# Q and K of the next batch inside the attention loop, scores in 64-row tiles with the mask as a matmul, and plain maxima

## What is computed

```python
xn = layernorm(x)
q, k, v = xn @ Wq + bq, xn @ Wk + bk, xn @ Wv + bv         # 16 heads of 16
scores = where(band & valid, q @ kc.T / 4, -1e9)            # 64 queries x 192 keys per block
a = softmax(scores) @ vc @ Wo + bo
h = layernorm(a + xn) * g1 + b1
t = layernorm(gelu(h @ W1 + c1) @ W2 + c2 + h) * g2 + b2
chosen = argmax(xn @ gate_w.T)
out = x + t + xn + xn @ expert_w[chosen].T
```

## Time and profile before

| | |
|---|---|
| three runs | 1550.31 us median, 1548.87 to 1557.77 |
| profiled execution, first to last instruction | 1553.1 us |
| TensorE busy | 1240.9 us, 80% |
| VectorE busy | 1071.5 us, 69% |
| ScalarE, GpSimd busy | 739.8 us, 739.9 us, 48% each |
| mean granted TensorE clock | 0.913 of full |
| DMA | 135 MB, mean 87 GB/s |

### The profile page before, as it was taken

The page is one execution under the profiler, slowest core; times in us unless marked ns, Lnnn a source line. Parts: engine busy times, 40 slices in busy tenths (PEclk is TensorE's granted clock), DMA queues, the critical chain, the costliest instruction groups (busy, mean ns, idle before and its releaser), DMA issues.

```text
span 1553.1 us, 34323 instructions
## 1 busy us (share of the span) xinstructions
PE 1240.9 (80%) x10696; PEld 714.8 (46%) x10696; DVE 1071.5 (69%) x3743; ACT 739.8 (48%) x1356; POOL 739.9 (48%) x749
## 2 busy tenths in 40 slices
PE   0648885999678985999859997689858898599967
PEld 0424452735346353654527454373535535265435
DVE  8656775777757775867757677576766676587565
ACT  1305744366543744447443565426544374445642
POOL 6443745156531766037550474406752177504661
PEclk9959997999989997989979899798988899799979
DMA  7463056220733119130462206422082212912010
GB/s 237 92 139 118 3 117 122 76 92 29 144 79 100 57 69 166 50 112 13 108 131 69 99 8 145 91 83 83 33 156 75 88 57 74 162 48 94 2 28 28
DMA packets 89647, 135.00 MB, mean 87 GB/s; under 512 B 10209, under 2 KB 62305, under 8 KB 87393
## 3 DMA queue, kind: packets, MB, share of 16 engines
q1 hardware_dynamic: 83328, 115.91, 30.0%
q0 software_dynamic: 6144, 16.79, 4.4%
HBM read 74.47 MB, written 59.90 MB: 87 GB/s over the span
## 4 chain that ended last, share of the span: by engine, by line
PE 49%; DMA 17%; issue 11%; POOL 8%; DVE 8%; SPq 3%; ACT 3%; DVEq 0%; POOLq 0%; ACTq 0%
DMA pair_dram<-pool 9%; PE bank L1132 8%; PE bank L1035 8%; PE bank L1154 8%; PE bank L1036 7%; PE bank L1038 7%; PE bank L1181 6%; DMA q_s<-q_s 5%; DVE xn L604 2%; SPq L284 2%; DMA ys_dram<-xn 2%; PE bank L1102 2%; POOL x_sb L453 2%; POOL x_sb L451 2%; POOL rs L386 2%
## 5 line engine op out<-in xcount | busy, mean ns | idle before, releaser
L713 DVE CUSTOM_DVE_ANT_0 bank<-bank,mask 128x192 f32<-128x192 f32 x1024 | 337.3, 388 | 199.1 <-PE bank L1132 195.1
L943 ACT ACTIVATE pool<-bank 128x512 f32<-128x512 f32 x512 | 293.0, 597 | 118.9 <-PE bank L1154 113.2
L1132 PE MATMUL bank<-k_s,q_s 128*64 128x192 f16 x2048 | 175.3, 269 | 144.1 <-DMA q_s<-q_s 141.2
L440 POOL TENSOR_SCALAR_AFFINE_SELECT pool<-pool 128x512 f32<-128x512 f32 x256 | 172.2, 675 | 194.1 <-ACT pool L943 193.4
L1154 PE MATMUL bank<-q_s,k_s 128*128 128x256 f16 x1024 | 199.3, 290 | 28.7 <-issue 21.3
L389 POOL TENSOR_TENSOR rs<-ve,neghalf 128x1 f32<-128x1 f32 x64 | 36.9, 577 | 384.8 <-DVE ve L776 384.8
L1132 PEld LDWEIGHTS bank<-k_s,q_s 128*64 128x64 f16 x2048 | 77.8, 113 | 250.1 <-issue 226.9
L1181 PE MATMUL bank<-pool,v_a 128*32 128x256 f32 (+2 forms) x2560 | 161.1, 345 | 19.9 <-DVE pool L727 8.6
L989 ACT ACTIVATE pool<-bank,c1c 128x512 f32<-128x512 f32 x128 | 87.8, 686 | 169.5 <-PE bank L1038 132.5
L790 DVE TENSOR_TENSOR pool<-pool 128x512 f16<-128x512 f32 x128 | 106.7, 839 | 63.3 <-ACT pool L955 62.2
L713 DVE DVE_READ_ACCUMULATOR2_ANT m_sb<- 128x1 f32 x1024 | 144.6, 141 | 0.3
(11 more groups left out here) (149 smaller groups left out, 2511.1 us busy)
## 6 DMA issues: line engine op xcount, KB each, us to landing
pair_dram<-pool SPq DMA_DIRECT2D x32, 512.0 KB, 7.6
xn<-xs_dram SPq DMA_DIRECT2D x40, 384.0 KB, 3.7
ys_dram<-xn SPq DMA_DIRECT2D x120, 128.0 KB, 1.7
q_s<-pair_dram SPq DMA_DIRECT2D x48, 256.0 KB
k_s<-pair_dram SPq DMA_DIRECT2D x48, 256.0 KB
x_sb<-in_L_attn_x SPq DMA_DIRECT2D x8, 1024.0 KB, 5.7
res_dram<-x_sb SPq DMA_DIRECT2D x8, 1024.0 KB, 4.8
res_r<-res_dram SPq DMA_DIRECT2D x8, 1024.0 KB, 7.4
```

The costliest lines, as they stand in the source:

```text
L440: nc.gpsimd.affine_select(out=p, in_=p, compare_op=ALU.is_ge, fill=0.0, base=0, pattern=[[0, 4], [1, 2 * W]], channel_multiplier=-1).then_ ...
L713: ins = nc.vector.tensor_tensor_reduce(out=SB[u % 2][:, i * WIN:i * WIN + WIN], in0=SB[u % 2][:, i * WIN:i * WIN + WIN], in1=mask[:, v, :] ...
L943: nc.scalar.activation(prob[:, (k + 2) % 3, 2 * pu:2 * pu + 2, :], TB[u % 2][:, :].rearrange("p (h q) -> p h q", h=2), ACT.Exp, scale=EXP_ ...
L1132: mm = nc.tensor.matmul(SB[u % 2][W * bl:W * bl + W, i * WIN:i * WIN + WIN], q_s[:, h, W + w0:2 * W + w0], k_s[:, h // 2, w0:w0 + WIN], st ...
```

## The change

- The x of the next batch is loaded in the previous turn (after the 11th sorted tile), its statistics stand in steps 0 to 4, the normalization in steps 8 to 11, its transposes in steps 11 to 14.
- Q and K of b + 1 are computed in steps 15 to 30: three of a unit's six matmuls in each step, between the two halves of the transposed scores; high part by ScalarE and low part by VectorE at every second step. They use two banks instead of four.
- The host permutes the columns of Wq, Wk and their biases; stores to pair_dram write every copy (12 of 256 KB instead of 4 of 512 KB), loads take 48 rows each (8 of 384 KB instead of 12 of 256 KB), in two halves by heads with a semaphore each. The copy of the row q_s<-q_s is gone.
- q_s holds two heads in 128 rows as k_s does. Scores and transposed scores contract over 48 or 64 rows; heads are grouped by row half (par) instead of by pair (pu). In a half step the transposed scores of one row half alternate with the scores of the other.
- The mask is added by two more matmuls for each half step (64 rows, 256 columns, from an identity), and the maximum is one plain reduction of 384 columns for two heads.
- The column transposes of the maxima use the banks of the scores, and wait for all maxima issued so far.

```diff
-    XN_AT = 23
+    XN_AT = 8
+    XT_AT = XN_AT + 3
+    QK_AT = XT_AT + 4
-    pair_dram = nc.dram_tensor("pair_dram", (2, 4, P, S), F16, kind="Internal").ap()
+    pair_dram = nc.dram_tensor("pair_dram", (2, 2, 4, 2, 3, HD, S), F16, kind="Internal").ap()
+    MAX_STEPS = [LEAD - T + 3] + [T * g + MAX_AT - 1 + LEAD for g in range(G - 2)]
-        q_s = sb("q_s", [P, H, S + 2 * W], F16)
+        q_s = sb("q_s", [P, H // 2, S + 2 * W], F16)
-        QB, VB = TB + MB, OB + TB
+        QB, VB = MB, OB + TB
...
+            def pair_stores(b, i):
+                c, qk = divmod(i, 2)
+                for src, done, slots in ((qk_h, qk_hi, (0, 2 if qk else 1)), (qk_l, qk_lo, (1 if qk else 2,))):
+                    sp.wait_ge(done.sem, done.at(b, 2 * i + 2))
+                    for slot in slots:
+                        sp.dma_start(pair_dram[c, qk, :, :, slot, :, :].rearrange("j a d s -> d (j a) s"),
+                                     src[:, 2 * qk + c, :]).then_inc(pair_st[i % 2].sem, 16)
+            def stack_loads(b, i, first=False):
+                c, qk = divmod(i, 2)
+                if not first and qk == 0:
+                    sp.wait_ge(ST_ps.sem, ST_ps.at(b - 1, 4 * T * (c + 1)))
+                    sp.sem_inc(passed, 1)
+                sp.wait_ge(pair_st[i % 2].sem, pair_st[i % 2].at(b, 48 * (i // 2 + 1)))
+                dst = k_s if qk else q_s
+                for a in range(2):
+                    sp.dma_start(dst[W * a:W * a + KW, 4 * c:4 * c + 4, W:W + S],
+                                 pair_dram[c, qk, :, a, :, :, :].rearrange("j o d s -> (o d) j s")).then_inc(stack[c].sem, 16)
...
+            def turn(b, last, x_next=True):
                 max_rows(b, 1)
+                load_res(b)
+                max_rows(b, 2)
                 if not last:
+                    pair_stores(b + 1, 0)
+                max_rows(b, 3)
                 if not last:
+                    pair_stores(b + 1, 1)
+                    for i in range(2):
+                        stack_loads(b + 1, i)
+                    for i in range(2, 4):
+                        pair_stores(b + 1, i)
+                    for i in range(2, 4):
+                        stack_loads(b + 1, i)
                     store_res(b + 1)
+                    sorted_tiles(b + 1, x_next)
                 store_out(b)
...
             def maxima(b, j):
+                for n, par in enumerate((1, 0)):
+                    dve.wait_ge(S_ps.sem, S_ps.at(b, 2 * j + n + 1))
+                    dve.sem_inc(passed, 1)
+                    nc.vector.tensor_reduce(m_sb[:, 4 * g + par:4 * g + 4:2, t],
+                                            SB[par][:, 0:2 * WIN].rearrange("p (h c) -> p h c", h=2), AX.X, ALU.max).then_inc(mx.sem, 1)
...
+            def score_mm(out, n, j, par, i):
+                g, t = divmod(j, T)
+                h, r = 2 * g + i, slice(W * par, W * par + KW)
+                q = W + (2 * t + n) * W
+                return nc.tensor.matmul(out[W * n:W * n + W, i * WIN:i * WIN + WIN], q_s[r, h, q:q + W], k_s[r, h, q - W:q + 2 * W],
+                                        start=i == 0, stop=False, skip_group_check=True)
...
+            def mask_mm(out, n, t, par):
+                r = slice(W * par, W * par + W)
+                band = mask[r, edge(2 * t + n), :, :].unsqueeze(1).broadcast_to([W, 2, 2, W])
+                dst = out[W * n:W * n + W, 0:2 * WIN].rearrange("p (h c k) -> p h c k", h=2, c=3)[:, :, 0::2, :]
+                return nc.tensor.matmul(dst, ident16[r, :], band, start=False, stop=True, skip_group_check=True)
...
+            def max_cols(b, g, issued):
+                pe.wait_ge(mx.sem, mx.at(b, 2 * issued))
+                nc.tensor.transpose(SB[g % 2][0:4 * T, 0:P], m_sb[:, 4 * g:4 * g + 4, :].rearrange("p h t -> p (h t)"),
...
+            def scores_t(b, k, par):
+                j = k - 1 + LEAD
+                both = 1 <= k and j < STEPS
...
+                if both:
+                    scores_wait(b, j, 1 - par)
                 for i in range(2):
+                    mt = score_t_mm(TB[par], k, par, i)
+                    if both:
+                        for n in range(2):
+                            score_mm(SB[1 - par], n, j, 1 - par, i)
+                mt.then_inc(ST_ps.sem, 1)
+                if both:
+                    for n in range(2):
+                        ms = mask_mm(SB[1 - par], n, j % T, 1 - par)
+                    ms.then_inc(S_ps.sem, 1)
...
             def turn(b, last):
                 for k in range(STEPS + LAG):
+                    for par in range(2):
                         if k < STEPS:
+                            scores_t(b, k, par)
+                        if par == 0 and XT_AT <= k < XT_AT + 4 and not last:
+                            xn_transposes(b + 1, k - XT_AT)
+                        if par == 0 and QK_AT <= k < QK_AT + 16 and not last:
+                            qk_half(b + 1, *divmod(k - QK_AT, 2))
                     if k >= LAG:
                         values(b, k - LAG)
```

More of the change, by code:

```diff
@@ L267, in load_x @@
                 sp.dma_start(x_sb[:, :, :], x_v[b]).then_inc(x_in.sem, 16)
-            def stacks(b):
[L271 to L288, removed]
@@ L499, in turn @@
                     band(b, k)
-                    if k == XN_AT - 1 and not last:
+                    if k == TH + 1 and not last:
                         rstd(b + 1, 0, ve0, rs0)
@@ L829, in turn @@
                         maxima(b, k - 1 + LEAD)
-                    if k == 2 * T + MAX_AT and not last:
+                    if k < TH and not last:
+                        for t in range(2):
+                            c1_tile(b + 1, 2 * k + t)
+                    if k == TH and not last:
                         c1_stage(b + 1)
@@ L848, in _ @@
             assert done == N_PREP_Z
+            for t in range(T):
+                c1_tile(0, t)
             c1_stage(0)
@@ L854, in _ @@
                 xn_low(0, u)
+            for u in range(8):
+                qk_low(0, u)
             dve.wait_ge(pprep.sem, N_PPREP_V)
@@ L1003, in _ @@
                 xn_high(0, u)
-            c2_stage(0)
+            for u in range(8):
+                qk_high(0, u)
             weights_b()
@@ L1048, in xn_transposes @@
                 pe.wait_ge(xn_rdy.sem, xn_rdy.at(b, TH * (u // DC) + TH))
-                if u == 0 and not first:
-                    pe.wait_ge(mT_ev.sem, mT_ev.at(b - 1, G))
                 if u >= 2:
@@ new lines, in scores @@
+            def scores(b, j, first=False):
+                for par in (1, 0):
+                    scores_wait(b, j, par, first)
+                t = j % T
+                for i in range(2):
+                    for n in range(2):
+                        for par in (1, 0):
+                            score_mm(SB[par], n, j, par, i)
+                for n in range(2):
+                    for par in (1, 0):
+                        mm = mask_mm(SB[par], n, t, par)
+                        if n == 1:
+                            mm.then_inc(S_ps.sem, 1)
@@ L1299, in _ @@
             pe.wait_ge(prep.sem, N_PREP_A)
+            for u in range(8):
+                for part in range(2):
+                    qk_half(0, u, part)
             c2_stage(0, True)
@@ L1350 @@
             a = a.transpose(0, 2, 1)
+        if name[8:] in ("Wq", "bq", "Wk", "bk"):
+            a = a.reshape(-1, P // HD, HD).swapaxes(1, 2).reshape(a.shape)
         if name[8:] in ("bq", "bk", "g1", "c1"):
```

227 lines of the change are left out of this document (114 added, 113 removed).

## The result

The changed kernel takes 1935.15 us (median of 4, 1910.83 to 1952.26), the kernel before 1552.62 us beside it (median of 4, 1548.87 to 1557.77). Two of the four runs (1947.54 and 1952.26 us) are slow ones and the ratio leaves them out: 1.2351, 95% interval 1.2289 to 1.2414. I had forecast 1484 us, range 1425 to 1600. The sign was wrong and the time lies far outside the range. The profiled execution (the run of 1922.77 us) has a span of 1921.0 us against 1553.1, and a mean granted clock of 0.752 against 0.913.

What follows compares the result with a forecast made beforehand. It took TensorE to bound the loop and the first scores' DMA wait to leave a hole behind it. Seven turns -56, last turn -6, prologue -4: -66 us from 1553.1, forecast 1484 us, range 1425 to 1600.

Steps and rivals of the forecast that it cites:

- The half step: In the attention loop: transposed scores (T) hide scores (S) on the opposite row half; 0.44 us against the present 0.61.
- my upper bound of 0.89: Half step in microseconds if every change of tile shape costs 0.10 us, including one from scores to masks.
- rival A: Loop: every tile-shape change is paid, also between row halves; half step 0.89 us, total 1609 us, slower; chance 0.27.
- B: Loop: shape changes half paid, 0.05 us each; half step 0.70, total about 1550 us, no change; chance 0.15.
- a fixed three steps: Loop steps 1 to 3 at the low clock: 0.74 us a half step against 1.00, 6 x -0.26 = -1.6 us.
- +13.9 us: Loop: normalization +4.1, transposes +1.5, Q and K +3.0 and +8.8, less 3.5 for work leaving the end.
- Steps 15 to 18: Loop: three Q and K products a step, 0.75 us with the change of shape; +3.0 us together.
- steps 8 to 14: Loop: next batch's normalization in steps 8 to 11, +4.1 us; transposes of x in steps 11 to 14, +1.5.
- the steps with Q and K alone: Loop steps 19 to 30: TensorE needs 1.97 us a step against 1.24 now, 12 x 0.73 = +8.8 us.
- Behind the loop: Loop end to W2: hole and QK products gone, GpSimd's adds hold VectorE; W2 starts 16 us earlier a turn.
- Rival C: Behind the loop: GpSimd's adds don't meet GELU's low parts; W2 9 us a turn earlier, total 1421 us; chance 0.12.
- -8 us a turn: Net of one turn: loop +8.7, behind the loop -16, W1 and W2 stages -0.5; seven turns -56 us.

Runs made afterwards that it cites:

- run 16: Changed kernel with transposed scores, scores and masks no longer interleaved; scores and masks over 128 rows, only transposed scores over 64: 1701.14 us.
- run 1: Changed kernel with each half step's two transposed scores issued first, then four scores, then two masks, still 64 and 48 rows: 1910.38 us, ratio 1.2264.
- run 2: Changed kernel with transposed scores, scores and masks not interleaved and all over 128 rows, zeros in the other head's rows: 1638.14 us, ratio 1.0517.
- run 13: Changed kernel without its new scores: Q and K in the loop, scores over 128 rows, masks on VectorE; 1571.29 us, ratio 1.0114.

## Why the prediction was wrong, point by point

**The half step, the step that failed.** "I take the lower: [...] those that share no part of the array start side by side", 0.44 us. It measured 1.46. Two errors lie in it. The first was the overlap: changes of shape are paid between row halves as well, four in a half step, and T hides nothing of S. A change costs nearly the same time at both levels, some 0.12 us: the kernel before has 0.61 and 1.00 us a half step, which is 0.37 and 0.75 for the columns and 0.24 and 0.25 for two changes, and run 16 shows the same. So at 2.4 GHz this half step would be 0.92 to 0.98 us, 0.48 of columns and 0.44 to 0.50 of changes; that is an estimate, as no run has this order at 2.4 GHz. It lies above my upper bound of 0.89 (whose terms add up to 0.91, with a change from S to M that doesn't exist): rival A came, not the forecast and not B, and by A's own sum this error alone makes the kernel slower. I had a row for column halves only the earlier trace rows and carried it over to rows. On this the Trainium skill's page "TensorEngine Tiling (Array Packing)" (Key Properties), with its drain at each change of mode, was the one that agrees with the trace, and I named it and took the other.
The second was not in the text at all: every term of the sum, both bounds and all the rivals held the loop's clock at 2.4 GHz from step 4 on. The low level of the first steps stood in the earlier trace rows and in the 0.89 of the earlier trace rows, and I priced it as a fixed three steps. In the changed kernel it lasts into steps 19 to 22 in five of the seven turns, into step 31 in the other two, and into step 23 in the last turn. Runs 1 and 2 price it: loops of 848.3 us with 64 and 48 rows, 563.8 with 128 rows and the same order, so 284 us. Why few rows keep the clock down no run shows. The interleaving costs another 62 us (910.2 to 848.3). The remaining 115 us of the +461 are those that run 2 has over the kernel before: the terms of Q and K, and the mask products.

**The rest of the loop.** Right in the main, once the half step is left out. I had put +13.9 us for normalization, transposes and Q and K less what leaves the end, and +1.5 for the maxima's transposes. In run 13, which has the half step of before, the loop takes 70.8 us against 57.8 in the fourth turn: +13. Steps 15 to 18 were put at +3.0 and cost 3.1; steps 8 to 14 at 5.6 together and cost 6.4 in four turns and 4.9 to 5.0 in three; the steps with Q and K alone at 1.97 and take 1.76 us in run 13 and 1.97 in the changed kernel, where two changes between 64 and 128 rows make the 0.21. The reduction of 384 columns was put at 0.56 us and takes 0.556.

**Behind the loop.** Right: W2 starts 66.9 us behind the loop's end, where 803.5 - 737.5 gave 66.0. nm takes 4.45 us as before, GELU begins 31.8 us behind the loop's end (31.3 forecast), and GpSimd's passes hold an operation of the routing for 4.03 us and low parts for 5.34 and 4.65 (two), as the price from the earlier trace rows had it. Rival C didn't come.
```profile
1217.10 4.03 DVE L701 TENSOR_TENSOR oh<-tiles,upto 128x64 f32<-128x64 f32 x1
...
1233.71 5.34 DVE L817 TENSOR_TENSOR pool<-pool 128x512 f16<-128x512 f32 x1 [0.60 <-ACT pool L991]
...
1239.90 4.65 DVE L817 TENSOR_TENSOR pool<-pool 128x512 f16<-128x512 f32 x2
```
Seven turns gave 93.5 us, forecast 112; most of the difference lies in the first three turns and the seventh, where it is 69.4 to 70.5 us and not 66.9.

**The prologue** was to be 4 us shorter by the smaller q_s, and is 0.4 shorter. The clearing did fall from 7.88 to 4.05 us and VectorE's first eight tiles from 26.5 to 22.0; what comes behind them took it back.

**The sum in hindsight.** Q and K in the loop cost 96.3 us in run 13's eight loops and gave 95.6 behind them; 11.8 more in the W2 stages and 5.1 in the prologue make the 1.1% by which it is slower. Nearly the whole forecast gain hung on the half step: of the -8 us a turn, 6.7 were the cheaper steps 1 to 18. Rival A had the changes of shape right; its 1609 us were still 326 short, since it too held the clock at 2.4 GHz.

**What stays open.** What decides at a loop's start if the clock falls and if it comes back: in run 16 it falls in seven turns and not in the last; in the changed kernel's last turn it falls too, although Q and K are missing there. And the release for which ScalarE waits on two of the chips.

## What to carry over

A change that cuts products into fewer rows is to be priced at both clock levels: see what level the stretch has before it and if it recovers within it, and put "it stays low" among the rivals with the doubled time for the columns; a change of shape costs some 0.12 us at either level here and isn't halved with them. Row halves aren't column halves: a row of the trace for one is no price of the other. And a pass of GpSimd beside a busy VectorE is best issued in pieces no longer than the wait that VectorE can afford; here that alone gave 1.7% in the kernel before, and 2.9% together with the MLP residual by tile and the change's one good part, Q and K in the loop.

## What the runs showed of the hardware that was not expected

- TensorE busy for 27.40 of 27.40 us at a granted clock of 0.50 (run 16), and 31.33 of 31.36 in the changed kernel. The Trainium skill's page "TensorE: Matmul & The Clock Gate" (Part 1: The HAM clock gate) has activity release the throttle and gives the full level for a busy TensorE. By that rule steps 4 to 11 would have run at 2.4 GHz; the measurement decides, and a busy TensorE isn't enough.
- One and the same stream of products holds 0.50 for 27.4 us and 1.00 for 22.0 us in one execution (run 16).
- Zeros are cheaper than empty rows: run 2 streams the same columns over 128 rows in 2.01 us a step, run 1 over 64 and 48 rows in 3.43.
- Two products that use opposite row halves, 64x128 and 64x64, did not run side by side: T to S 0.32 us, S to T 0.31 at 1.2 GHz.
- A change of tile shape between two products cost 0.10 to 0.14 us at 1.2 GHz and 0.10 to 0.13 at 2.4 GHz (run 16's T to V: 1.21 and 0.71 us, of which 0.96 and 0.48 are columns).
- The same kernel took 1610.19 us on one chip and 1571.29 on another, where the kernel before differed by 6 us; each chip had only one set of runs.
